# A selective-scan kernel: one B product in four moved from DVE to POOL, and other slots for jobs in the queues of DVE, ACT and PE

## What is computed

```python
xb = jax.nn.silu(conv(x_br))
Bm = xb @ W_b ; Cm = xb @ W_c
delta = jax.nn.softplus(xb @ W_delta + b_delta)
A_bar = jnp.exp(delta[..., None] * A)
Bx = delta[..., None] * Bm[:, :, None, :] * xb[..., None]
h = a_t * h + bx_t                     # over time, for every channel and state
y_t = jnp.sum(h * c_t[:, None, :], axis=-1)
out = (y + xb * Dp) * jax.nn.silu(z) @ W_out
```

## Time and profile before

| | |
|---|---|
| median of 3 runs | 2885.6 us |
| the profiled execution | 2885.02 us |
| its span, first to last instruction | 2883.0 us |
| first scan starts | 114.0 us |
| last scan ends | 2361.5 us |
| one block, mean of blocks 1 to 14 | 140.0 us |
| DVE, PE, POOL, ACT busy in one block | 125.1, 117.0, 97.8, 86.3 us |

### The profile page before, as it was taken

One profiled execution on the slowest core, in us unless ns is written; L12 is line 12 of the kernel. 1 busy time (PEld: TensorE's weight loads), 2 busy tenths in 40 slices (PEclk: granted clock), 3 DMA queues, 4 the chain that ended last, 5 costly groups with the idle time before them and its releaser, 6 DMA issues. The chain is left out here.

```text
span 2883.0 us, 38176 instructions
## 1 busy us (share of the span) xinstructions
PE 2396.6 (83%) x11520; PEld 1642.8 (57%) x11520; DVE 2378.5 (83%) x2438; ACT 1675.9 (58%) x3282; POOL 1682.5 (58%) x1993
## 2 busy tenths in 40 slices
PE   7878878788878888888888888888888794899997
PEld 5556656565656565666665666565656331444443
DVE  2489898898898988898888898898989664688887
ACT  2565656565757565657575656565656444555654
POOL 0266667676767676767676767676767550222221
PEclk8888999998999898999999999999988896999999
DMA  4101010201020201010110101010102531121110
GB/s 171 66 2 68 7 70 5 71 5 70 5 71 5 74 13 63 16 59 31 45 51 24 60 16 60 15 63 13 60 8 89 205 139 71 55 66 55 65 59 23
DMA packets 47510, 152.50 MB, mean 53 GB/s; under 512 B 7973, under 2 KB 8869, under 8 KB 44206
## 3 DMA queue, kind: packets, MB, share of 16 engines
q1 hardware_dynamic: 47278, 149.76, 14.4%
HBM read 132.37 MB, written 17.37 MB: 52 GB/s over the span
## 5 line engine op out<-in xcount | busy, mean ns | idle before, releaser
L451 POOL TENSOR_TENSOR ring<-ring,Cbc 128x512 f32<-128x512 f32 x1024 | 1292.1, 1283 | 44.2
L841 DVE TENSOR_TENSOR_SCAN ring<-a_ps,ring 128x1024 f32<-128x1024 f32 x512 | 1165.2, 2278 | 50.8 <-ACT a_ps L658 50.4
L658 ACT ACTIVATE a_ps<-delta,nA 128x255 f32<-128x255 f32 x2048 | 851.0, 465 | 452.7 <-DVE ring L841 450.5
L1038 PE MATMUL yT_ps<-ident,ring 128*128 128x128 f32 x4096 | 606.4, 291 | 234.4 <-POOL ring L451 224.3
L1038 PEld LDWEIGHTS yT_ps<-ident,ring 128*128 128x128 f32 x4096 | 486.5, 148 | 360.2 <-POOL ring L451 315.2
L833 DVE TENSOR_TENSOR ring<-u_ps,Bbc 128x1024 f32<-128x1024 f32 x512 | 619.9, 1211 | 45.0 <-PE yT_ps L1038 38.9
L1004 PE MATMUL work<-xb,big 128*128 128x256 f32 x2048 | 487.0, 394 | 0.0
L444 POOL TENSOR_TENSOR carry<-ring,half 128x4 f32<-128x4 f32 x512 | 146.5, 286 | 581.7 <-DVE ring L841 579.3
L1004 PEld LDWEIGHTS work<-xb,big 128*128 128x128 f32 x2048 | 398.7, 200 | 54.3 <-issue 0.4
L977 PE MATMUL work<-y0s,big 128*128 128x256 f32 x1024 | 243.6, 396 | 0.7 <-issue 0.7
L1020 PE MATMUL work<-Wout,xb 128*128 128x512 f32 x512 | 239.5, 606 | 0.0
(11 more groups left out here) (194 smaller groups left out, 2697.4 us busy)
## 6 DMA issues: line engine op xcount, KB each, us to landing
Bbc<-bc_rows SPq DMA_DIRECT2D x64, 512.0 KB, 4.5
Cbc<-bc_rows SPq DMA_DIRECT2D x64, 512.0 KB, 3.9
xT<-in_xT SPq DMA_DIRECT2D x16, 514.0 KB, 3.3
x_rows<-x2row SPq DMA_DIRECT2D x32, 256.0 KB, 2.0
xp<-x_rows SPq DMA_DIRECT2D x32, 256.0 KB, 2.7
xx<-in_x SPq DMA_DIRECT2D x32, 256.0 KB, 3.0
out_rows<-orow SPq DMA_DIRECT2D x32, 256.0 KB, 2.0
delta<-in_c_w SPq DMA_DIRECT2D x6, 1024.0 KB, 4.9
```

What stands on the lines that cost most here:

```text
L451: nc.gpsimd.tensor_tensor(hp, hp, Cbc[:, G * g + GP * c:G * g + GP * c + GP, :], ALU.mult)\
L658: r = nc.scalar.activation(a_ps[q % 2][:, i, 1:T], delta[:, par, dt, 1:T], ACT.Exp, scale=nA[:, dt, s:s + 1])
L841: dve.tensor_tensor_scan(ring[:, q % RING, :, :].rearrange("p g t -> p (g t)"), a_ps[q % 2][:, :, :].rearrange("p g t -> p (g t)"), ring[: ...
L1038: r = pe.matmul(yT_ps[:, tt, :], ring[:, q % RING, i, P * tt:P * tt + P], ident[:, :], is_transpose=True, start=False, stop=(g == NG - 1 a ...
```

## The change

Three things are done. **The product moves:** u * B of the last group of each channel tile (q % 4 = 3, ring place 3) is made by POOL in a new function `last_bx`. POOL runs it in the first slot of the channel tile, behind the product with C of that slot. It makes its own copy of u in SBUF (`u_sb`) first, since it reads no PSUM here. DVE's `bx` returns at once for that group, and its scan waits for POOL (`s_bxp`). **Column 0:** DVE waits for POOL's last product before it writes column 0 of B for the next channel tile; for channel tile 0 the columns of groups 2 and 3 are written together in slot 1. The load of the next block's B of group 3 waits for POOL. **Small ones:** the scan of the first model writes to PSUM and not to `st0`, and its bank is given free by a memset behind it, one DVE instruction more a block. Many jobs get other slots: on PE `wo(1)` goes from slot 8 to 6, the four pairs of `x` from 11-14 to 12-15, z one slot later, `dl(2)` and `dl(3)` are spread over 24 to 31; on DVE `stats(0)` from 7 to 6, `dmin(1)` from 4 to 3, `dmax(1)` from 6 to 7; ACT's jobs follow PE's.

```diff
+NBX = ND * (NG - 1)
+        u_sb = spare[:, 512:512 + T]
@@ SyncE
                     sp.wait_ge(s_col0, NCOL * NBLK)
+                    sp.wait_ge(s_bxp, ND * NBLK)
                     def bload(g):
-                        if scan:
-                            sp.wait_ge(s_bx, NQ * n - NG + g + 1)
+                        if scan and g < NG - 1:
+                            sp.wait_ge(s_bx, NBX * (n - 1) + NBX - NG + 1 + g + 1)
+                        elif scan:
+                            sp.wait_ge(s_bxp, ND * n)
@@ POOL
+            def last_bx(k, dt, par):
+                delta_ready(pool, k, dt)
+                wait(pool, s_bxp, ND * k + dt)
+                nc.gpsimd.tensor_tensor(u_sb[:, 1:T], delta[:, par, dt, 1:T], xb[:, par, dt, 1:T], ALU.mult)\
+                    .then_inc(s_up, 1)
+                if isinstance(k, int) and k == 0 and dt == 0:
+                    pool.wait_ge(s_uone, 1)
+                if dt == 0:
+                    pool.wait_ge(s_bl[NG - 1], 16 * k + 16)
+                pool.wait_ge(s_col0, NCOL * k + NG + dt)
+                wait(pool, s_tr, NQ * k + NG * dt)
+                pool.wait_ge(s_up, ND * k + dt + 1)
+                nc.gpsimd.tensor_tensor(ring[:, RING - 1, :, :],
+                                        u_sb.rearrange("p (a t) -> p a t", a=1).to_broadcast([P, G, T]),
+                                        Bbc[:, NS - G:NS, :], ALU.mult).then_inc(s_bxp, 1)
...
                         nc.gpsimd.tensor_tensor(hp, hp, Cbc[:, G * g + GP * c:G * g + GP * c + GP, :], ALU.mult)\
                             .then_inc(s_hc, 1)
+                    if g == 0:
+                        last_bx(k, dt, par)
@@ ACT
-                next_plan = {5: [prj], 6: [prj_ln], 10: [y0scale], 11: [y0back], 14: [lambda: xcopy(0)],
-                             15: [lambda: xcopy(1)], 16: [lambda: xcopy(2)], 17: [lambda: xcopy(3), silu],
-                             18: [lambda: zcopy(0), lambda: zcopy(1)], 19: [lambda: zcopy(2), lambda: zcopy(3)],
-                             21: [zsilu], 22: [bc], 24: [lambda: dexp(0, False)], 25: [lambda: dexp(1, False)],
-                             26: [lambda: dln(0, False)], 32: [lambda: dexp(2, False)]}
-                scan_plan = {3: [lambda: dexp(3, True)], 6: [lambda: dln(1, True)]}
-                turned = {13: 0, 20: 1, 28: 2}
+                next_plan = {5: [prj], 6: [prj_ln], 12: [y0scale], 13: [y0back], 15: [lambda: xcopy(0)],
+                             16: [lambda: xcopy(1)], 17: [lambda: xcopy(2)], 18: [lambda: xcopy(3), silu],
+                             19: [lambda: zcopy(0)], 20: [lambda: zcopy(1), lambda: zcopy(2)], 21: [lambda: zcopy(3)],
+                             22: [bc], 23: [zsilu], 24: [lambda: dexp(0, False)], 26: [lambda: dexp(1, False)],
+                             27: [lambda: dln(0, False)], 30: [lambda: dexp(2, False)]}
+                scan_plan = {1: [lambda: dexp(3, True)], 6: [lambda: dln(1, True)]}
+                turned = {14: 0, 21: 1, 28: 2}
@@ DVE, scan0
-                    dve.tensor_tensor_scan(st0[:, :], sc0[0:N0, 3:4].to_broadcast([N0, T]), ps[0:N0, T:2 * T],
-                                           carry0[:, fp:fp + 1], ALU.mult, ALU.add).then_inc(free[BANK["PRJ"]], 1)
+                    dve.tensor_tensor_scan(ps[0:N0, T:2 * T], sc0[0:N0, 3:4].to_broadcast([N0, T]), ps[0:N0, T:2 * T],
+                                           carry0[:, fp:fp + 1], ALU.mult, ALU.add).then_inc(s_sc0, 1)
...
-                    dve.scalar_tensor_tensor(y0[0:N0, :], st0[:, :], sc0[0:N0, 1:2], c0[:, :],
+                    dve.scalar_tensor_tensor(y0[0:N0, :], ps[0:N0, T:2 * T], sc0[0:N0, 1:2], c0[:, :],
                                              ALU.mult, ALU.mult).then_inc(s_c0, 1)
+                    dve.wait_ge(s_c0, base + 5)
+                    dve.memset(mark[:, :], 0.0).then_inc(free[BANK["PRJ"]], 1)
@@ DVE, bx
+                    if g == NG - 1:
+                        return
...
+                        if g == NG - 2:
+                            dve.wait_ge(s_bl[g + 1], 16 * k + 16)
+                            dve.tensor_reduce(Bbc[:, G * g + G:G * g + 2 * G, 0], first[:, 0, G * g + G:G * g + 2 * G]
+                                              .rearrange("p (s o) -> p s o", o=1), AX.X, ALU.add).then_inc(s_col0, 1)
                     elif g == 0:
+                        dve.wait_ge(s_bxp, ND * k + dt)
                         dve.tensor_reduce(Bbc[:, :, 0], first[:, dt, :].rearrange("p (s o) -> p s o", o=1), AX.X, ALU.add)\
                             .then_inc(s_col0, 1)
@@ DVE, scans and plans
-                    dve.wait_ge(s_bx, NQ * k + q + 1)
+                    if g < NG - 1:
+                        dve.wait_ge(s_bx, NBX * k + (NG - 1) * dt + g + 1)
+                    else:
+                        dve.wait_ge(s_bxp, ND * k + dt + 1)
...
-                next_plan = {4: [gates0], 5: [scan0], 7: [lambda: stats(0)], 8: [lambda: stats(1), stats_end],
+                next_plan = {4: [gates0], 5: [scan0], 6: [lambda: stats(0)], 8: [lambda: stats(1), stats_end],
-                scan_plan = {4: [lambda: dmin(1, True)], 6: [lambda: dmax(1, True)]}
+                scan_plan = {3: [lambda: dmin(1, True)], 7: [lambda: dmax(1, True)]}
@@ PE, plan
-                        5: [("n", wo, 0), ("b", wout, 0, 1)], 6: [("b", wout, 0, 2)],
-                        7: [("b", wout, 1, 0)], 8: [("n", wo, 1), ("b", wout, 1, 1)],
-                        9: [("b", wout, 1, 2), ("n", turn_y0)], 10: [("n", turn_back)],
-                        11: [("s", turn_gated, 0, k), ("n", x, 0, 0), ("n", x, 0, 1)],
-                        12: [("n", x, 1, 0), ("n", x, 1, 1)], 13: [("n", x, 2, 0), ("n", x, 2, 1)],
-                        14: [("n", x, 3, 0), ("n", x, 3, 1)], 15: [("n", z, 0), ("n", z, 1)], 16: [("n", z, 2)],
-                        17: [("n", z, 3)], 18: [("s", turn_gated, 1, k)], 19: [("n", bc)],
+                        5: [("n", wo, 0), ("b", wout, 0, 1)], 6: [("b", wout, 0, 2), ("n", wo, 1)],
+                        7: [("b", wout, 1, 0)], 8: [("b", wout, 1, 1)],
+                        9: [("n", turn_y0), ("b", wout, 1, 2)], 10: [("n", turn_back)],
+                        11: [("s", turn_gated, 0, k)], 12: [("n", x, 0, 0), ("n", x, 0, 1)],
+                        13: [("n", x, 1, 0), ("n", x, 1, 1)], 14: [("n", x, 2, 0), ("n", x, 2, 1)],
+                        15: [("n", x, 3, 0), ("n", x, 3, 1)], 16: [("n", z, 0), ("n", z, 1)], 17: [("n", z, 2)],
+                        18: [("n", z, 3), ("s", turn_gated, 1, k)], 19: [("n", bc)],
...
-                        26: [("s", turn_gated, 2, k), ("n", dl, 2, 0)], 27: [("n", dl, 2, 1)],
-                        28: [("n", dl, 2, 2), ("n", dl, 2, 3)], 29: [("n", dl, 3, 0)],
-                        30: [("n", dl, 3, 1), ("n", dl, 3, 2)], 31: [("n", dl, 3, 3)]}
+                        24: [("n", dl, 2, 0)], 25: [("n", dl, 2, 1)],
+                        26: [("s", turn_gated, 2, k), ("n", dl, 2, 2)], 27: [("n", dl, 2, 3)],
+                        28: [("n", dl, 3, 0)], 29: [("n", dl, 3, 1)], 30: [("n", dl, 3, 2)], 31: [("n", dl, 3, 3)]}
```

More of the change, by code:

```diff
@@ L182, in scan_phase @@
         s_c0 = sem("s_c0")
+        s_sc0 = sem("s_sc0")
         s_y0k = sem("s_y0k")
@@ L212, in scan_phase @@
         s_bx = sem("s_bx")
+        s_bxp = sem("s_bxp")
+        s_up = sem("s_up")
+        s_uone = sem("s_uone")
         s_a = sem("s_a")
@@ L431, in step @@
                             r.then_inc(s_cpow, 1)
+                    if isinstance(k, int) and k == -1 and q == 20:
+                        pool.wait_ge(s_mz, 2)
+                        nc.gpsimd.memset(u_sb[:, 0:1], 1.0).then_inc(s_uone, 1)
                     if not scan:
@@ L621, in step @@
                     dt, g = q // NG, q % NG
-                    if scan and q == FIRST[1] + 2:
+                    if scan and q == FIRST[1] + 3:
                         first_exp(1, k)
-                    if front and q == FIRST[0] + 2:
+                    if front and q == FIRST[0] + 3:
                         first_exp(0, k + 1)
@@ L719, in scan0 @@
                     dve.wait_ge(s_c0, base + 3)
-                    dve.tensor_tensor_scan(st0[:, :], sc0[0:N0, 3:4].to_broadcast([N0, T]), ps[0:N0, T:2 * T],
-                                           carry0[:, fp:fp + 1], ALU.mult, ALU.add).then_inc(free[BANK["PRJ"]], 1)
-                    dve.wait_ge(free[BANK["PRJ"]], jobs_before("PRJ", k) + 1)
-                    dve.tensor_copy(carry0[:, fp:fp + 1], st0[:, T - 1:T]).then_inc(s_c0, 1)
-                    dve.scalar_tensor_tensor(y0[0:N0, :], st0[:, :], sc0[0:N0, 1:2], c0[:, :],
+                    dve.tensor_tensor_scan(ps[0:N0, T:2 * T], sc0[0:N0, 3:4].to_broadcast([N0, T]), ps[0:N0, T:2 * T],
+                                           carry0[:, fp:fp + 1], ALU.mult, ALU.add).then_inc(s_sc0, 1)
+                    dve.wait_ge(s_sc0, n + 1)
```

(12 more changed lines are left out.)

1 line of the change is left out of this document (removed).

## The result

The changed kernel takes 2906.1 us, the median of seven runs (2893.2 to 2912.4), beside 2885.6 of the kernel before. The ratio is 1.0065, with a 95% interval of 1.0043 to 1.0086: it is slower by 0.65%, where 2791 us were forecast. The profiled execution has a span of 2907.3 us.

The account below looks back on a forecast made before the run. POOL would become the longest engine, with PE's surplus in three tiles: blocks fall from 140.0 to 134.0 us. Fifteen blocks save 90, block 15 saves 3, the prologue 1: 2791 us, own range 2735 to 2840, chance 0.62.

Parts of the forecast that it names:

- Moves with one answer: Step on the moved jobs and extra waits: nothing counted for spreading dl(2) and dl(3), x one slot later taken as covered.
- The sum: Whole kernel: fifteen blocks x 6.0 us, 3 for block 15 and 1 for the prologue, together 94 us less.
- Its cover is the slots until `dl`: Claim that x, starting one slot later, has the slots until dl as slack; no cost counted in the forecast.
- POOL's 15.6 us each: Every channel tile: POOL as longest engine sets the pace, its work and its meetings with DVE included.
- the surpluses: PE work beyond POOL's time, less 2 us in hand: 4 us lost in tile 1, 1.7 each in tiles 3 and 5.
- The term of the product: Product moved from DVE to POOL: 8.7 us a block off DVE, 3.2 us a channel tile added to POOL.
- The chain by hand: Timing of one channel tile from T, POOL always busy: scan(3) ends at T + 10.2, 1.8 us in hand.
- tile 1's wait of the statistics: DVE's wait for PE's wo(1): 4.9 us a block would go; tile 1 would be longest, 18 to 20 us.
- the lower bound of 2.4: Duration of POOL's new product: 2.50 us forecast, 2.4 if one start is saved, 2.8 at most.
- The meetings of DVE and POOL: Operations with two SBUF inputs on both engines hold each other up: 1.6 us a block, bounds 0 and 4.
- rival 3: Slot 1's product, turn and ring place come 3.2 us later, lengthening tiles; 143.2 us a block, 2933 us; chance 0.10.

Follow-up runs that it names:

- product_dl: Changed kernel with the x, y0, z, bc and silu jobs of slots 9 to 23 and dmax back in their former places; 2818.5 us, ratio 0.9763.
- pool_load: Kernel before, plus one 128x256 and two 128x512 POOL operations nobody waits for, behind the C product of each tile's first slot; 2958.7 us.
- product_only: Changed kernel with the former job places on PE, ACT and DVE; product on POOL and y0 scan in PSUM stay; 2909.6 us, ratio 1.0086.
- wo_dl: Kernel before with wo(1) and stats(0) early, y0 scan in PSUM and new dl(2), dl(3) places with their exps and min; 2785.0 us.
- own_column: Changed kernel, but POOL writes column 0 of B for its own group and DVE's reduction no longer waits for POOL's last product; 2919.7 us.
- short_product: Changed kernel, but POOL's product covers only the first 16 of 256 steps, leaving out work; all waits and the copy of u stay; 2803.9 us.
- x_as_before: Changed kernel with y0's scaling, the four pairs of x and their ACT copies back in the slots of before; 2842.4 us, ratio 0.9853.
- pe_no_loop: Changed kernel with PE's program written out for all blocks, without its loop; 2898.6 us, ratio 1.0038.
- cload_late: Changed kernel, but the next block's C loads for groups 2 and 3 also wait for PE's last turn of the block; 2888.7 us.

## Why the prediction was wrong

**The step that failed: "Moves with one answer", where the moved jobs were counted at nothing.** Only `wo(1)` and `stats(0)` had a term, 4.9 us a block, which measured 58 and 60 us in all, against 74. The dl places, with y0 in PSUM, gave 44 us without the product, for 12 counted. The places of slots 9 to 23 took 88 us. The sum had nothing for them but 1.7 us a block, 25 us in all, for four pairs of x in tile 3. "Its cover is the slots until `dl`" was said of x's products, but the cover asked for was that of the turns between them: a turn waits for all jobs written ahead of it. Without these places the time is 2818.5 us (`product_dl`), about 28 over the forecast.

By tiles, the forecast comes to POOL's 15.6 us each and the surpluses: 19.6 for tile 1, 17.3 for tiles 3 and 5, 15.9 for the others. Tiles 1, 5 and 7 came within 0.3 us of that, tile 2 stayed 1.6 under it. What the forecast of the block lacked is in tiles 0 (2.4 us over), 3 (2.3), 4 (3.1) and 6 (1.7).

**The term of the product had the wrong sign.** It costs 24 us with the old places and 21 with `wo` early (in both against a kernel without `scan0` in PSUM), 33 with dl as well and 63 with all (both against a kernel that has it). It is the difference of two effects: `pool_load` shows 72 us for keeping POOL busy at that place, `product_only` is 49 us under it, with DVE's relief and `scan0` in PSUM in it; since the load was 2.7 us a tile and product and copy are 3.1, this split is an estimate. The forecast worked out DVE's 8.7 and the 3.2 us of POOL rightly enough (in blocks 1 to 14 DVE is busy for 118.5 us a block where 115.6 were forecast, 2.2 of the difference in `dmax` and `dmin`, and POOL for 121.6 where 123.4 were), and then took the longest engine for the bound. It wasn't: POOL is idle for 20 us a block.

Tile 5 shows what was missed. It takes 16.1 us in `wo_dl` and in `product_dl`, to the tenth, though DVE does one product less. DVE in `wo_dl` (product on DVE), then in `product_dl`:

```profile
1271.06 2.28 DVE L844 TENSOR_TENSOR_SCAN ring<-a_ps,ring 128x1024 f32<-128x1024 f32 x1
1273.26 0.41 DVE L818 TENSOR_TENSOR u_ps<-delta,xb 128x255 f32<-128x255 f32 x1
1274.23 0.18 DVE L833 TENSOR_REDUCE Bbc<-big 128x16 f32<-128x16 f32 x1 [0.56 <-PE yT_ps L1041]
```
```profile
1285.70 4.46 DVE L884 TENSOR_TENSOR_SCAN ring<-a_ps,ring 128x1024 f32<-128x1024 f32 x2
1290.08 0.53 DVE L850 TENSOR_TENSOR u_ps<-delta,xb 128x255 f32<-128x255 f32 x1
1292.69 0.18 DVE L870 TENSOR_REDUCE Bbc<-big 128x16 f32<-128x16 f32 x1 [2.08 <-PE yT_ps L1081]
```

and PE in the same two places:

```profile
1265.96 7.07 PE L1007 MATMUL work<-xb,big 128*128 128x256 f32 x32
...
1273.09 1.04 PE L1041 MATMUL yT_ps<-ident,ring 128*128 128x128 f32 x8
```
```profile
1284.44 7.07 PE L1047 MATMUL work<-xb,big 128*128 128x256 f32 x32
...
1291.56 1.04 PE L1081 MATMUL yT_ps<-ident,ring 128*128 128x128 f32 x8
```

DVE gains 1.1 us by two scans in a row (4.46), and waits 1.5 us longer for the turn of slot 20. PE runs the dl jobs of two slots, 7.07 us, between the turns of slots 19 and 20, because the first slot of a tile has its turn ahead of its jobs and all others behind them. Where that stretch sets the tile, DVE's relief is worth nothing. **The chain by hand left this stretch out.** It let bx(4) wait for POOL's product only, at T + 6.5, with scan(3) done at T + 10.2, and so found 1.8 us in hand; the turn that frees the ring place for bx(4) isn't in it. The trace of the changed kernel in tile 3 (block 8, T = 1300.5 us) has it: two pairs of x, then the turn of slot 12, which ends at T + 10.3. DVE's reduction waits 3.65 us for it, scan(3) ends at T + 14.0, and POOL, which asks at T + 12.1, waits 2.01 us:

```profile
1301.48 8.20 PE L1020 MATMUL work<-y0s,big 128*128 128x256 f32 x32
...
1309.74 1.04 PE L1081 MATMUL yT_ps<-ident,ring 128*128 128x128 f32 x8
```
```profile
1310.87 0.18 DVE L870 TENSOR_REDUCE Bbc<-big 128x16 f32<-128x16 f32 x1 [3.65 <-PE yT_ps L1081]
```
```profile
1314.59 0.20 POOL L473 TENSOR_TENSOR carry<-ring,half 128x4 f32<-128x4 f32 x1 [2.01 <-DVE ring L884]
```

The sum then took PE's surplus as absorbed once a tile, while late x also made ACT's copies and silu late in the next.

**Right in the forecast:** tile 1's wait of the statistics is gone and the tile takes 19.5 us, within 18 to 20, though tile 3 with 19.6 is as long; the product's duration (2.36 us, just under the lower bound of 2.4); that DVE's reduction on `s_bxp` costs nothing with the product in the first slot (`own_column`). The meetings of DVE and POOL exist: in the changed kernel `dmax` takes 1785 ns for 1195 and `dmin` 1287 for 793,

```profile
L802 DVE TENSOR_TENSOR delta<-delta,lnbuf 128x1024 f32<-128x1024 f32 x25 | 44.6, 1785 | 0.0
L795 DVE TENSOR_SCALAR lnbuf<-lnbuf 128x1024 f32<-128x1024 f32 x26 | 33.5, 1287 | 16.5 <-ACT lnbuf L604 16.5
```

2.2 us a block on DVE, which has idle time; `pool_load` shows a loss without them, though with longer u.

**The rivals.** The time came out on the side of rival 3, the late chain. Its mechanism is there (`pool_load`, `short_product`), but its price was wrong: 3.2 us a tile from 4.5 tiles on; measured are 4.8 us a block for 2.7 us a tile. Without the late x the chain would not have made the changed kernel slower: `x_as_before` is 44 us under the kernel before.

**Two causes that no rival had.** The first is what happens at the jump of the loops: the six blocks behind a jump take 2.8 us longer than the even ones, about 17 us in all. PE's part of it can't be the whole, since these blocks stayed as long without PE's loop.

The second is the clock granted to TensorE. The first job of a block takes 5.16 to 5.30 us in all even blocks and in block 1 of the changed kernel, 3.62 or 3.63 in every block of the kernel before. Wherever it takes 3.62 or 3.63 in an even block of `pe_no_loop` (three of seven) or `cload_late` (five of seven), tile 0 takes 15.2 us, and elsewhere 16.6, as in all even blocks of the changed kernel. Tile 0 of blocks 4 and 8 of `pe_no_loop`, first the columns of the earlier trace rows with the clock ahead of the last two figures, then the job:

```profile
679.60:695.60 16.00, 13.06 (x66) 9.58 (x66) 14.25 (x15) 8.48 (x22) 15.03 (x17) 0.89 0.32 109
1246.00:1262.00 16.00, 11.61 (x66) 8.36 (x66) 15.90 (x16) 10.02 (x25) 15.27 (x17) 1.00 0.36 112
```
```profile
682.88 5.25 PE L958 MATMUL work<-xT,Wtap 128*128 128x256 f32 x16
```
```profile
1249.22 3.63 PE L958 MATMUL work<-xT,Wtap 128*128 128x256 f32 x16
```

So in even blocks 1.4 us of tile 0 are the clock, and this is the gain that even blocks show there with the late C loads and without PE's loop. In tile 3 the two pairs of x above took 8.20 us for 7.08 in the earlier trace rows; in the same even blocks of `pe_no_loop` that have the fast first job, tile 3 takes 18.1 us for 19.7. By the clock's records of blocks 1 to 14, 25.4 us of a block are at the lower level in the changed kernel, 22.2 before, 19.0 in `product_dl` and 18.3 in `x_as_before`. A part of the 88 us is therefore this and not the order alone; how large a part, no run separates.

**Still open.** Why the clock is granted otherwise at one start of a block than at another. How much of the stops at the jump the C loads cause. How far `short_product`'s 102 us are the chain and how far the shorter meetings with DVE. The two best variants, 2780.4 and 2785.0 us, are both faster than the kernel before and the changed one, and are not told apart.

## What to carry to other kernels

Where several engines pass pieces through a few places, as here, the time of a stretch can be set by the longest piece of work that stands between two hand-overs in one queue, and not by the busy time of an engine; before work is taken off the busiest engine, read who releases its next instruction once it is done earlier. Count each moved job by what stands behind it in its queue, and try moves one by one: three entries gave 58 us, a few more 31 to 44, and a group of others took 88 back, all in one change. Idle time of an engine is free only at the places where nobody waits for what comes after it.

## What was not expected of the hardware

In the blocks behind a jump of the loops PE is idle for 4.3 to 5.2 us and POOL for 4.1 to 5.9 in the changed kernel, for 0.7 to 1.4 and 1.7 to 2.0 in the kernel before. Written out without its loop, PE shows none of it. The Trainium skill (Runtime: NRT & Kernel Launch, section "Instruction fetch mechanics") says that a taken branch to a page that isn't at hand forces a fetch before execution goes on; the runs agree for PE that there is a stop, but don't show what is fetched in it. I expected the stop to grow with transfers in flight, and this is partly borne out: with the C loads later PE's stop was 3.3 to 3.5 us.

The granted clock of TensorE fell at the start of blocks. In the changed kernel, two stretches of 2 us at the start of block 9, while PE had nothing to do, and in the kernel before, two across the start of block 7:

```profile
1388.00:1390.00 2.00, 0.00 (x0) 0.00 (x0) 1.95 (x4) 1.45 (x4) 0.62 (x1) 0.77 0.68 256
1390.00:1392.00 2.00, 0.25 (x1) 0.26 (x2) 0.00 (x0) 0.21 (x1) 0.00 (x0) 0.50 0.56 215
```
```profile
1096.00:1098.00 2.00, 1.31 (x12) 1.07 (x11) 2.00 (x2) 0.00 (x0) 0.58 (x1) 1.00 0.46 164
1098.00:1100.00 2.00, 2.00 (x15) 1.84 (x13) 1.97 (x5) 1.92 (x5) 1.73 (x3) 1.00 0.04 8
```

At 0.50, the level of 1.2 GHz, the first job of block 7 took 5.17 us, for 3.62 before. But this isn't the price of the stop: in block 8, where PE had stood idle for 0.57 to 0.85 us at a time only, the clock fell as well (0.89 over the first 16 us of the block) and the job took as long:

```profile
1247.59 0.66 PE L1081 MATMUL yT_ps<-ident,ring 128*128 128x128 f32 x4 [0.85 <-POOL ring L480]
1248.82 0.84 PE L1081 MATMUL yT_ps<-ident,ring 128*128 128x128 f32 x4 [0.57 <-POOL ring L480]
1249.45 5.16 PE L958 MATMUL work<-xT,Wtap 128*128 128x256 f32 x16
```
